# Group norm by small stationary tiles and a first norm turned over DRAM, in layer 2 of a four-layer attention program

## The reference

```python
# layer 2, per sequence: x is [l, 512], 32 heads of 16 channels
xa = _ln(x, ln1_w, ln1_b)                                 # first norm, per token
sx = concat([state[:, 1:2] - xa[:, :1], xa[:, :-1] - xa[:, 1:]], axis=1)
xxx = tanh((xa + sx * maa_x) @ maa_w1)                    # five mixing factors
xk, xw, xv, xr, xg = (xa + sx * (maa_stack + xxx @ maa_w2))
w, r, k, v, g = ...                                       # decay and projections
out = scan(step, s0, (r, k, v, w))                        # 16 x 16 state for each head
og = out.reshape(b, l, 32, 16)
og = (og - mean(og)) / sqrt(var(og) + 1e-5)               # group norm: groups of 16 channels
x1 = x + (og * gn_w + gn_b) * g @ Wo.T
xc = _ln(x1, ln2_w, ln2_b)                                # then a shift and a gated feed-forward
# layer 3
scores = q @ k.T / 4 + mask; out = softmax(scores) @ v @ Wo + x, then a layer norm
```

## Time and profile before

| what | value |
|---|---|
| median of 3 runs | 2152.98 us (2150.59 to 2153.21) |
| the profiled execution | 2149.68 us, of which its span 2147.8 us |
| TensorE (PE) busy | 2083.7 us, 97% of the span |
| VectorE (DVE), ScalarE (ACT), GpSimd (POOL) busy | 55%, 51%, 26% |
| mean granted clock of TensorE | 0.990 |

### The profile page before, as it was taken

One profiled execution on the slowest core, in us unless ns is written; L12 is line 12 of the kernel. 1 busy time (PEld: TensorE's weight loads), 2 busy tenths in 40 slices (PEclk: granted clock), 3 DMA queues, 4 the chain that ended last, 5 costly groups with the idle time before them and its releaser, 6 DMA issues. The chain is left out here.

```text
span 2147.8 us, 56309 instructions
## 1 busy us (share of the span) xinstructions
PE 2083.7 (97%) x21720; PEld 1509.2 (70%) x21720; DVE 1184.7 (55%) x3285; ACT 1098.9 (51%) x3380; POOL 556.7 (26%) x573
## 2 busy tenths in 40 slices
...
GB/s 170 183 146 73 136 104 109 107 107 108 107 109 108 108 108 108 108 108 91 88 156 18 63 57 51 52 50 68 63 57 49 51 53 65 66 55 50 51 62 36
DMA packets 219264, 185.84 MB, mean 87 GB/s; under 512 B 93888, under 2 KB 177216, under 8 KB 216768
## 3 DMA queue, kind: packets, MB, share of 16 engines
...
...
## 5 line engine op out<-in xcount | busy, mean ns | idle before, releaser
L881 PEld LDWEIGHTS bank<-normedT,mlp_w 128*128 128x128 f32 x2048 | 232.6, 193 | 11.0 <-issue 9.9
L881 PE MATMUL bank<-normedT,mlp_w 128*128 128x128 f32 x2048 | 238.5, 278 | 0.8 <-DVE normedT L1168 0.8
L891 PE MATMUL bank<-mlp_w,geluT 128*128 128x512 f32 x480 | 208.5, 592 | 0.0
L2396 ACT ACTIVATE scores_turned<-scores_turned,nmax 128x128 f32<-128x128 f32 x480 | 185.4, 392 | 21.2 <-DVE nmax L2653 21.2
L891 PEld LDWEIGHTS bank<-mlp_w,geluT 128*128 128x128 f32 x480 | 90.1, 190 | 107.5 <-issue 107.5
L1865 POOL TENSOR_TENSOR k_even_odd<-k_even_odd,decay_products 128x512 f32<-128x512 f32 x80 | 94.0, 1174 | 271.2 <-PE quad L2067 130.1
L1118 DVE CUSTOM_DVE_ANT_0 probs<-quad,neg_mask 128x256 f32<-128x256 f32 x256 | 90.8, 421 | 94.3 <-PE quad L832 94.3
L2553 DVE COPY_PREDICATED wkv_scores<-level_masks,quad 128x1024 f32<-128x1024 int32 x64 | 99.5, 1554 | 64.3 <-PE quad L2072 40.5
L1014 ACT ACTIVATE probs<-probs,nmax 128x256 f32<-128x256 f32 x256 | 126.6, 496 | 8.1 <-DVE nmax L1118 7.4
L2653 DVE CUSTOM_DVE_ANT_0 scores_turned<-quad,mask 128x128 f32<-128x128 f32 x480 | 104.1, 287 | 40.5 <-PE quad L2186 40.4
L695 POOL COPY latents_b<-latents_b_next 128x512 f32<-128x512 f32 x16 | 9.8, 610 | 443.1 <-DVE l_x L1177 404.4
...
## 6 DMA issues: line engine op xcount, KB each, us to landing
l_blocks<-probs_turned_blocks SPq DMA_DIRECT2D x124, 256.0 KB, 2.7
...
x_in<-l_out SPq DMA_DIRECT2D x32, 256.0 KB, 3.6
x_in<-in_x SPq DMA_DIRECT2D x16, 256.0 KB, 2.7
ctx_in<-in_ctx SPq DMA_DIRECT2D x16, 256.0 KB, 2.9
```

The costliest lines, as they stand in the source:

```text
L881: mm = nc.tensor.matmul(ps[:, f * P:(f + 1) * P], mlp_w1[:, c, m * P:(m + 1) * P], nT[:, c, :], start=(c == 0), stop=(c == NC - 1))
L891: mm = nc.tensor.matmul(PS[u.bank][:, :], gT[:, f, :], mlp_w2[:, f, :], start=(f == 0), stop=(f == NF - 1))
L2396: ac = nc.scalar.activation(s, s, ACT.Exp, bias=nmax[:, k, 2 * c + e:2 * c + e + 1], scale=-1.0, accum_out=rsum[:, kv, gr:gr + 1])
```

## The change

The first norm is no longer turned by TensorE. VectorE turns `ln1_x` in blocks of 32x32 within its partitions (`n_turn`, into the tile `sx`, which is free then), a DMA stores it in DRAM (`n_put`), and four DMAs bring it back with the blocks in their places (`n_back`, into `ln1_x` itself). ScalarE reads it from there into `xaT`.

The group norm changes its tiles. `w_var` now holds the stationary tile small: `gn_sums_at`, 128x32, which is placed in each of the array's four groups of 32 columns, and the squares of 32 tokens are the moving tile; 16 matmuls instead of 4. Its output has 32 groups for each 32 tokens. `w_rep` multiplies by a pattern to 128x128 numbers instead of copying to 128x512, and `w_rstd` is 4 matmuls of 32x128 stationary tiles, each into another bank of the quad, instead of 4 transposes into a single bank. VectorE makes the patterns once (`x_setup2`). All tables are new. Here is the diff, without most of the tables:

```diff
-        grr, gated, kk, nx2 = sq, sq, sq, flat(dev)
+        grr, gated, kk, nx2 = flat(sq)[:, 0:P], sq, sq, flat(dev)
...
-                ("w_var",): (7, 1), ("w_rstd",): (6, 1), ("w_out",): (5, 1), ("w_xc",): (5, 1), ("w_fk",): (5, 1), ("w_fr",): (5,
...
+                1), ("p_level", 5): ("quad", 1), ("p_level", 6): ("quad", 1), ("p_s0",): (5, 1), ("w_var",): (5, 1), ("w_rstd",):
+                ("quad", 1), ("w_out",): (7, 1), ("w_xc",): (6, 1), ("w_fk",): (7, 1), ("w_fr",): (7, 1), ("w_fv",): (6, 1),
...
+        def blocks(t):
+
+            return t.rearrange("p (c m t) -> p c m t", m=NC, t=SB)
+
+        def turned_blocks(t):
+
+            return t.rearrange("p (m c t) -> p c m t", m=NC, t=SB)
+
+        def moved(t, c):
+
+            return t.rearrange("p (q c t) -> p q c t", c=NC, t=SB)[:, :, c, :]
...
+                def put(k, src, s_put):
+                    sp.dma_start(blocks_out[k].rearrange("p m c t -> p (m c t)"), src).then_inc(s_put, 16)
+
+                def back(k, dst, s_back):
+                    for m in range(NC):
+                        sp.dma_start(dst[SB * m:SB * m + SB, :].rearrange("f (q x) -> f q x", q=RG),
+                                     blocks_out[k][:, m, :, :].rearrange("(q f) c t -> f q (c t)", f=SB)).then_inc(s_back, 16)
+
+                def n_put(i, uses):
+                    sp.wait_ge(s_nblk, i)
+                    put("n", flat(sx), s_nput)
+
+                def n_back(i, uses):
+                    sp.wait_ge(s_nput, 16 * i)
+                    back("n", nx[:, :], s_nback)
...
-                    nc.gpsimd.tensor_copy(flat(grr).rearrange("p (h j) -> p h j", j=D2), grs[:, :].unsqueeze(2).to_broadcast([P, H2, D2]))\
-                        .then_inc(s_grr, 1)
...
+                    nc.gpsimd.tensor_tensor(grr.rearrange("p (c t) -> p c t", t=SB), grs[:, :].unsqueeze(1).to_broadcast([P, NC, SB]),
+                                            chunk_of_row[:, 0:NC].unsqueeze(2).to_broadcast([P, NC, SB]), ALU.mult).then_inc(s_grr, 1)
...
-                def n_xa(i, uses):
-                    pe.wait_ge(s_nx1, i + 1)
-                    turn4(uses[("n_xa",)], uses[("n_xa",)].psum, nx)
...
                     for c in range(NC):
-                        mm = nc.tensor.matmul(PS[b][:, HC * c:HC * (c + 1)], sq[:, c, :], hsum[:, :], start=True, stop=True)
+                        for r in range(RG):
+                            rr = slice(SB * r, SB * r + SB)
+                            mm = nc.tensor.matmul(PS[b][rr, 0:SB], sums_at[:, c, :], sq[:, c, rr], start=(c == 0), stop=(c == NC - 1))
...
-                    for c in range(NC):
-                        mm = nc.tensor.transpose(PS[b][:, c * P:(c + 1) * P], flat(grr)[:, c * P:(c + 1) * P], ident[:, :])
+                    for r in range(RG):
+                        rr = slice(SB * r, SB * r + SB)
+                        mm = nc.tensor.matmul(PS[r][:, 0:P], groups_wide[rr, :], grr[rr, :], start=True, stop=True)
...
+                def scaled_blocks(dst, t, w, b, s_done):
+                    for c in range(NC):
+                        ac = nc.scalar.activation(dst[:, c, 1:P + 1].rearrange("p (q t) -> p q t", t=SB), moved(t, c), ACT.Identity,
+                                                  bias=C(b, c), scale=C(w, c))
+                    ac.then_inc(s_done, 1)
...
+                def n_turn(i, uses):
+                    dve.wait_ge(s_nx1, i + 1)
+                    dve.sem_inc(s_hold, 1)
+                    dve.wait_ge(s_mixed, NM * i)
+                    dve.sem_inc(s_hold, 1)
+                    nc.vector.transpose(turned_blocks(flat(sx)), blocks(nx[:, :])).then_inc(s_nblk, 1)
...
-                    u, ps = use(uses, "w_rstd")
-                    nc.vector.tensor_tensor(dev[:, :, :], dev[:, :, :], chunked(ps[:, :]), ALU.mult).then_inc(u.free, 1)
+                    u = uses[("w_rstd",)]
+                    made(u)
+                    d = dev[:, :, :].rearrange("p c (r t) -> p c r t", t=SB)
+                    nc.vector.tensor_tensor(d, d, quad[:, 0:RG, 0:P].rearrange("p r (c t) -> p c r t", t=SB), ALU.mult).then_inc(u.free, 1)
```

More of the change, by code:

```diff
@@ new lines, in layers23 @@
+        USES = {("p_t5",): (7, 1), ("p_t5t",): (7, 1), ("p_mix",): ("quad", RG), ("p_mix4",): ("quad", 1), ("p_u1",): (5, 1),
+                ("p_w",): (5, 1), ("p_k",): (7, 1), ("p_r",): (6, 1), ("p_v",): (7, 1), ("p_g",): (5, 1), ("p_level", 0): ("quad",
+                1), ("p_level", 1): ("quad", 1), ("p_level", 2): ("quad", 1), ("p_level", 3): ("quad", 1), ("p_level", 4): ("quad",
+                1), ("p_level", 5): ("quad", 1), ("p_level", 6): ("quad", 1), ("p_s0",): (5, 1), ("w_var",): (5, 1), ("w_rstd",):
+                ("quad", 1), ("w_out",): (7, 1), ("w_xc",): (6, 1), ("w_fk",): (7, 1), ("w_fr",): (7, 1), ("w_fv",): (6, 1),
+                ("a_x",): (6, 1), ("a_q",): (6, 1), ("a_kv",): (5, 1), ("a_score", 0): ("quad", RG), ("a_score", 1): ("quad", RG),
+                ("a_norm",): (5, 1), ("b_out",): (7, 1)}
@@ new lines, in layers23 @@
+        ORDER = dict(
+            pe=[("p_t5",), ("a_x",), ("w_var",), ("p_t5t",), ("p_mix",), ("b_out",), ("a_q",), ("p_mix4",), ("a_kv",), ("w_rstd",),
+                ("p_k",), ("a_score", 0), ("p_u1",), ("p_r",), ("a_score", 1), ("p_w",), ("w_out",), ("p_level", 0), ("p_g",),
+                ("p_level", 1), ("w_xc",), ("p_v",), ("p_level", 2), ("w_fk",), ("p_level", 3), ("w_fv",), ("p_level", 4),
+                ("w_fr",), ("p_level", 5), ("a_value", 0), ("a_norm",), ("p_level", 6), ("a_value", 1), ("p_s0",), ("p_av",),
+                ("p_av6",)],
+            act=[("p_t5",), ("p_t5t",), ("a_x",), ("p_xm", 0), ("p_xm", 3), ("p_xm", 2), ("p_xm", 1), ("p_xm", 4), ("a_q",),
+                 ("a_kv",), ("w_rstd",), ("p_k",), ("b_store",), ("a_exp", 2), ("a_exp", 3), ("p_u1",), ("p_r",), ("a_exp", 1),
+                 ("a_exp", 0), ("p_w",), ("a_exp", 4), ("a_exp", 7), ("a_exp", 5), ("a_exp", 6), ("w_xc",), ("n_xa",), ("p_v",),
+                 ("w_fk",), ("p_g",), ("w_fr",), ("a_norm",), ("p_level6",), ("a_bias",), ("p_wkv",)],
+            dve=[("n_ln1",), ("w_var",), ("n_nx",), ("b_out",), ("p_s0c",), ("p_xm", 0), ("b_ln",), ("p_xm", 3), ("w_rstd",),
+                 ("p_xm", 1), ("p_xm", 4), ("p_xm", 2), ("a_max", 2), ("a_max", 3), ("a_max", 0), ("a_max", 1), ("n_turn",),
+                 ("w_gate",), ("a_max", 5), ("a_max", 7), ("a_max", 6), ("a_max", 4), ("a_turn", 0), ("w_out",), ("p_rup", 0),
+                 ("p_merge", 0), ("a_turn", 1), ("a_turn", 2), ("w_ln2",), ("p_rup", 1), ("p_merge", 1), ("a_turn", 3), ("w_sx",),
+                 ("w_xk",), ("a_turn", 4), ("p_merge", 2), ("a_rinv",), ("a_turn", 5), ("p_rup", 2), ("a_turn", 6), ("a_turn", 7),
+                 ("p_merge", 3), ("p_rup", 3), ("p_gate",), ("w_xr",), ("p_rup", 4), ("p_merge", 4), ("n_shift",), ("p_merge", 5),
+                 ("p_rup", 5), ("p_rup", 6), ("w_fv",), ("a_norm",)],
+            pool=[("n_first",), ("n_rstd",), ("w_pow",), ("b_rstd",), ("w_rep",), ("p_xm", 0), ("p_xm", 3), ("p_xm", 1),
+                  ("w_first",), ("p_xm", 2), ("a_x3b",), ("p_xm", 4), ("p_k0",), ("p_s0b",), ("p_ur",), ("p_wl",), ("p_kup", 0),
+                  ("w_rstd2",), ("p_kup", 1), ("p_kup", 2), ("p_kup", 3), ("a_norm",), ("p_kup", 4), ("p_kup", 5)],
+            sp=[("n_put",), ("n_ldx",), ("n_lds0",), ("n_back",), ("w_lda",), ("a_move", 0), ("a_move", 1), ("a_move", 2),
+                ("a_move", 3), ("p_v",), ("a_move", 4), ("a_move", 5), ("a_move", 7), ("a_move", 6), ("p_ldw",)])
```

297 lines of the change are left out of this document (147 added, 150 removed).

## The result

| | before | after |
|---|---|---|
| time, median (range) | 2153.10 us (2150.59 to 2154.86, 4 runs) | 2166.35 us (2161.30 to 2168.89, 4 runs) |
| profiled execution: time, span | 2149.68, 2147.8 us | 2161.30, 2159.5 us |
| TensorE busy in the span | 2083.7 us, 97% | 2081.0 us, 96% |

The ratio is 1.0064, 95% interval 1.0049 to 1.0079: the changed kernel is slower by 0.64%. The forecast was 2152.0 us with a range up to 2162, and gave "slower by over 0.2%" a chance of 0.33. TensorE is busy for 2.7 us less, and the span of the profiled execution is 11.7 us longer.

The account below looks back on a forecast made before the run. TensorE, never idle in steady steps, was taken as the bound: 2149.68 - 12.8 (slots) + 10.1 (steady waits) + 1.7 (ends) = 2148.7 us profiled, with 3.3 more for the median 2152.0; range 2142 to 2162.

Parts of the forecast that it names:

- slower by over 0.2%: Whole kernel: slower by over 4.3 us, through dearer `w_var`, worse ends or late DMAs; chance 0.33.
- The slots: TensorE: `n_xa` gone (0.49 us), `w_var` 0.28 and `w_rstd` 0.06 cheaper for each batch; 12.8 us saved in all.
- `w_var` is dearer: Rival at `w_var` on TensorE: passes cost more than neighbouring rows show, 2159.4 us at twice, 2171.8 without overlap; chance 0.14.
- The wait at `p_mix`: TensorE between `p_t5t` and `p_mix`: without `a_kv` as cover it waits for ScalarE's `t5T` copy, 0.66 us a step.
- Level 6: TensorE ahead of level 6: without `n_xa` it waits for VectorE's `p_merge` 5 and `p_rup` 5, 0.18 us a step.
- 0.14 to notice: VectorE ahead of level 6: time from level 5's end until it starts, 0.14 us of the 1.69 us sum.
- in either order of the two: VectorE ahead of level 6: `p_merge` 5 and `p_rup` 5 take 1.69 us from level 5's end, whichever comes first.
- 0.10 behind and 0.04 ahead: TensorE at `w_var`: return to full tiles 0.10 us and entry 0.04, within its forecast slot of 0.60.
- ahead of `w_var`(1): Head: `w_var` of batch 1, directly behind the recurrence, waits 0.14 + 0.60 us for the squares.
- at the quad: Head: `a_score` behind `w_rstd` of batch 1 waits for VectorE to empty the quad, some 0.14 + 0.7 us.
- the ends, by some 5 us: Rival in head and tail: new tables shift waits either way, 2147 or 2157 us; chance worse 0.12, better 0.10.
- The new transfers: SP's queue: `n_put` and `n_back` add five issues, 3.5 us, costed at nothing; rival of late DMAs, chance 0.07.

Follow-up runs that it names:

- e5: Changed kernel with its new order, but the group norm (`w_var`, `w_rep`, both `w_rstd`) in the form of before; 2165.63 us, ratio 1.0064 to the kernel before.
- e3: Changed kernel with `a_kv` back between `p_t5t` and `p_mix` and `w_rstd` behind `p_k` in steady steps; 2172.28 us, ratio 1.0094 to the kernel before.
- e6: Kernel of e3 with `p_xm` 0 ahead of the output norm on VectorE and GpSimd; 2156.93 us, ratio 1.0028 to the kernel before.
- e2: Changed kernel with `p_rup` 5 ahead of `p_merge` 5 on VectorE in the steady order; 2161.33 us, ratio 1.0040 to the kernel before.
- e1: Changed kernel with `n_ln1`(2) and `n_rstd`(2) moved behind three mixing products of batch 1 in the head; 2154.54 us, ratio 1.0017 to the kernel before.
- e9: Changed kernel with the load `n_ldx`(1) ahead of `p_v`(0) and the weights in SP's head queue; 2159.94 us, ratio 1.0032 to the kernel before.
- e12: Changed kernel with the load `n_ldx`(1) between `p_v`(0) and the weights in SP's head queue; 2154.73 us, ratio 1.0018 to the kernel before.
- e7: Changed kernel with `b_out` between `p_t5t` and `p_mix` in TensorE's steady order, `a_kv` left in place; 2175.66 us, ratio 1.0114 to the kernel before.
- e13: Changed kernel with e12's head and e11's steady order; 2149.23 us, ratio 0.9987 to the kernel before.
- e14: Changed kernel with e1's head and e11's steady order; 2148.84 us, ratio 0.9982 to the kernel before.
- e11: Changed kernel with e9's head, e6's steady order and e2's exchange on VectorE; 2150.97 us, ratio 0.9992 to the kernel before.

## Why the prediction was wrong

**The slots** (forecast 12.8 us saved) came out better: 0.49 + 0.49 + 0.10 a step in place of 0.49 + 0.28 + 0.06. The rival "`w_var` is dearer" is refuted: 32 passes in 0.39 us are 12 ns each. The Trainium skill (page TensorE: Matmul & The Clock Gate, section "Wait — 56ns, not 53.3ns?") gives a floor of about 25 ns from start to start; by it, an estimate, the 32 passes would take 0.80 us. The trace disagrees for passes in four column tiles side by side.

**The wait at `p_mix`** was right in place, cause and price: 0.66 forecast, 0.75 measured, in every steady step (e5, with no tiled group ahead of `p_t5t`, has 0.73). e3 and e6 take it away. e6 keeps the cover and its step is 0.49 us shorter than the changed kernel's, level 4 left out.

**Level 6** was right in place and too small: 0.18 forecast, 0.40 measured. The term that failed is "0.14 to notice", and that the sum holds "in either order of the two". Where the merge comes first VectorE starts 0.28 behind the slot (e2: 0.14 with `p_rup` 5 first), and the way to level 6 is 1.93 us, not 1.69 to 1.71. With `p_rup` 5 first it is 1620.37 - 1618.63 = 1.74 in e2, and the wait 0.21, close to the forecast. Set against the 0.49 of `n_xa`, moving the first norm off TensorE is worth 0.09 us a step here (0.28 in e2's order), since what it had covered came to light.

**What the sum left out** in the steady step: the price that tiled groups put on their neighbours. The forecast took 0.10 behind and 0.04 ahead inside `w_var`'s slot, and 0.04 inside `w_rstd`'s, and read no other group's new neighbours; these come to 0.33 a step. e5 measures 0.09 to 0.10 for a full group ahead of a tiled one as well as behind, and two tiled groups have two sides each. 0.42 saved at `w_var` is 0.12 net.

Steady step in all: forecast -0.83 + 0.84 = 0.0 us, measured -1.08 + 1.15 + 0.33 = +0.40, 4.8 us in twelve; the rest of the 5.5 in the table is the order of the tail in the twelfth distance. Against the forecast the slots saved 0.25 more, the waits cost 0.31 more, and the neighbours cost 0.33.

**The head** is where the prediction failed outright. It priced two waits, ahead of `w_var`(1) (0.74) and at the quad (0.84), and both came, at 0.81 each:

```profile
1173.35 0.46 PE L2157 MATMUL bank<-gn_squares,gn_sums_at 128*32 128x32 f32 x32 [0.81 <-ACT gn_squares L2378]
1182.36 1.15 PE L2224 MATMUL quad<-k_even_odd,ffn_r_in 32*128 32x256 f32 x16 [0.81 <-DVE gn_dev L2643]
```

It left everything else to the rival "the ends, by some 5 us". SP's queue was read only for the issues that were added (`n_put`, `n_back`), not for what had changed places in it: `n_ldx`(1) had gone from ahead of the weights to behind them, and `n_ln1`(2) on VectorE stood ahead of work that TensorE needs. e1, e9 and e12 show the mechanism from three sides. By the times the load is worth more than the 5.5 us of the one profile: e1 and e12, which differ from the changed kernel in the head alone, are both 10 us faster. The new transfers themselves cost nothing, as forecast, and the tail's +1.1 us is within what the rival allowed for the ends.

So the time lies beyond the range because two effects add up, the head's 5.5 to 10 us, a case that was held at 0.12, and the steady steps' 4.8. What stays open is the rest: the profiled execution of the changed kernel was the fastest of its four, 5 us below their median, and of the 10 us that e1 wins only 6 can be read. What the other executions waited for isn't seen, beyond the longer wait that e2 to e7 have at the same place. In the changed orders (e13, e14) the loss is gone with the head's repair and e11's steady order together.
